# First attention of a two-layer decoder: the small matrix work of an iteration set beside the P*V products

## The chip, the cores and the metric

One NeuronCore of a Trainium2 chip runs the whole program. The metric is the device time of one execution in microseconds (us). Engines: TensorE (PE, matmuls; its weight loads are listed as PEld), VectorE (DVE), ScalarE (ACT), GpSimd (POOL), SyncE (SP, which here only issues DMAs).

## The reference

Eight sequences of 256 tokens with 128 channels go through two pre-norm layers of self-attention, cross-attention and a feed-forward part. The change touches the very first block, self-attention with 16 heads of 8 channels:

```python
x = x + _L0_attn_ref(_layernorm(x, axis=-1), W_qkv, b_qkv, W_out, b_out)
...
qkv = x @ W_qkv.T + b_qkv
q, k, v = jnp.split(qkv, 3, axis=-1)          # each to (B, 16 heads, 256, 8)
scores = jnp.einsum('bhqd,bhkd->bhqk', q, k) / jnp.sqrt(jnp.float32(HEAD_DIM))
att = jax.nn.softmax(scores, axis=-1)
out = jnp.einsum('bhqk,bhkd->bhqd', att, v)
return out.transpose(0, 2, 1, 3).reshape(B, T, D) @ W_out.T + b_out
```

The rest (cross-attention with one head, an expert block, causal attention, a second 16-head attention on the context, and a routed feed-forward part with a top-k) is the same in both kernels and runs after it.

## The kernel before

Every engine has its own program, written out by hand; nothing is scheduled by a tool. Semaphores tie them together. The kernel has three stages. The first 16-head attention (`lo == 0` in the code) goes over eight items, one sequence each. A middle stage does cross-attention, experts and causal attention. The second 16-head attention (`lo == B`) has the same loop as the first, over eight more items.

The loop of a 16-head attention is `for i ...: for h in range(16)`, and each engine walks it in the same order. At head h of iteration i TensorE issues, in `both_scores`, two kinds of scores turn by turn: the second scores of item i (L1324, `scores`, with the row maxima already folded in as an extra row of the stack) and the first scores of item i + 1 (L1333, `scores_for_max`), from which VectorE takes the maxima (L954, `row_max`). Both are bf16 matmuls on 62 or 63 rows of the array. The second scores of a head fill one of two banks and ScalarE's exponential (L658, `exps`) empties it; the first scores have three banks. These are the waits of the scores in `both_scores`, c and d being running numbers of heads:

```python
pe.wait_ge(exp_ready, c - 1)      # exponential of head h - 2 is done
pe.wait_ge(max_ready, d - 2)      # maxima of head h - 3 are done
```

Between the heads stands the rest of TensorE's work, in fp32:

- P*V (`weighted_sum`, L1370), 8 matmuls for four heads, each on 32 columns of the array: groups 0, 1, 2 at heads 5, 9, 13, group 3 at head 1 of the next iteration.
- For the item x = i + 3 that is being prepared: the transposes of its normalised input (`xn_transpose`, L1272), its q and k projections (`qk_project`, L1280 and L1284), its v projection (`v_project`, L1307). x runs from 3 to 9; items 8 and 9 already belong to the cross-attention and have only q (L1280).
- The transposes of the maxima (`max_transpose`, L1318), twice per item, at head 3 and for the next item at head 10.
- For item i - 1: transposes of the P*V result (`u_transpose`, L1383, head 3), of the normalised output (`o_transpose`, L1389, head 11), and the output projection (`out_project`, L1401, head 15).

ScalarE's list is, besides the exponentials: `max_copy` (L694) and the DMA that places the maxima in the stack (`place_max`, L700), `xnT_copy` (L668), `qk_copy` (L681), `v_copy` (L715), `u_copy` (L706), `oT_copy` (L752). `max_transpose`, `xn_transpose`, `qk_project` and `v_project` share one bank, `prep_ps`: each waits (`prep_free`) until ScalarE has copied the one before. After `qk_copy`, GpSimd splits q and k into bf16 parts and SyncE places them in the stack for iteration i + 2.

The heads at which these steps stand are numbers in the `if h == ...` lines. `at(lo, first, second)` gives one number for the first attention and another for the second.

Of the kernel before, what the change touches and what calls it, by code (L numbers as in the profile page):

```python
# [35 lines left out]
B, S, D = 8, 256, 128  # L36
# [39 lines left out]
CROSS, CAUSAL, LAST = 1, 2, 3  # L76
# [13 lines left out]
def build(nc, t):  # L90

    ctx = ExitStack()
    with ctx:
# [189 lines left out]
        def has(n, lo):  # L283

            return lo <= n < lo + B

        def layer(n):

            return WORK[n][0]
# [33 lines left out]
        def slot(n):  # L323

            return 2 if WORK[n][0] == LAST and n < MID_END else n % 2

        def before(n):

            return max((j for j in range(n) if slot(j) == slot(n)), default=None)

        def at(lo, first, second):

            return second if lo else first
# [318 lines left out]
        def _(act):  # L652
# [138 lines left out]
            for lo in MANY:  # L791
# [33 lines left out]
                for i in steps_of(lo):  # L825
                    x = prepared(i, lo)
                    for h in range(H):
                        if has(i, lo):
                            exps(i, h)
                        if h == 1 and has(i - 1, lo):  # L830
                            u_copy(i - 1)
                        if h == 3 and has(i, lo) and i != B:
                            max_copy(i, 1)
                        if h == 4 and has(i, lo) and i != B:
                            place_max(i, 1)
                        if h == at(lo, 3, 5) and x is not None:
                            xnT_copy(x)
                        for _ in range(KV_AT.get(i, ()).count(h)):
                            kv_copy(kv_done)
                            kv_done += 1  # L840
                        if h == at(lo, 7, 8) and x is not None:
                            qk_copy(x)
                        if (i, h) == (-3, 7):
                            value_biases()
                        if h == 11 and has(i + 1, lo):
                            max_copy(i + 1, 0)
                        if h == 12 and has(i + 1, lo):
                            place_max(i + 1, 0)
                        if h == 11 and has(i - 1, lo):
                            oT_copy(i - 1)  # L850
                        if h == 15 and x is not None and has(i + 3, lo):
                            v_copy(i + 3)
                        if h == 0 and lo == B and has(i - 3, lo):
                            xrT_copy(i - 3 - B)
# [404 lines left out]
        def _(pe):  # L1259
# [126 lines left out]
            def o_transpose(n):  # L1386
                pe.wait_ge(o_ready, n + 1)
                for k in range(NT):
                    i = pe.transpose(out_ps[:, k * P:(k + 1) * P], o_tok[:, n % 2, k, :], ident[:, :])  # L1389
                i.then_inc(oT_psum, 1)  # L1390
# [123 lines left out]
            for lo in MANY:  # L1514
# [55 lines left out]
                for i in steps_of(lo):  # L1570
                    x = prepared(i, lo)
# [7 lines left out]
                    for h in range(H):  # L1579
# [18 lines left out]
                            prep_free = (maxT_ready, 2 * i + 2)  # L1598
                        if h == 3 and has(i - 1, lo):
                            u_transpose(i - 1)  # L1600
                        if lo == 0 and h == 4 and x is not None:
                            if prep_free:
                                pe.wait_ge(*prep_free)
                            xn_transpose(x)
                            prep_free = (xnT_ready, x + 1)
                        if h % G == 1 and h >= G and has(i, lo):
                            weighted_sum(i, h // G - 1)
                        if lo == B and h == 5 and x is not None:
                            if prep_free:
                                pe.wait_ge(*prep_free)  # L1610
                            xn_transpose(x)
                            prep_free = (xnT_ready, x + 1)
                        if h == at(lo, 7, 8) and x is not None:
                            qk_project(x)
                            prep_free = (qk_ready, 2 * (x + 1))
                        if (i, h) == (-3, 7):
                            fold_matmul(0)
                        if (i, h) == (B - 1, 7) and lo == 0:
                            pe.wait_ge(*prep_free)
                            fold_matmul(1)  # L1620
                            prep_free = (bias_folded, 2)
                        if h == 11 and has(i - 1, lo):
                            o_transpose(i - 1)
                        if h == 10 and has(i + 1, lo):
                            if prep_free:
                                pe.wait_ge(*prep_free)
                            max_transpose(i + 1, 0)
                            prep_free = (maxT_ready, 2 * (i + 1) + 1)
                        for _ in range(KV_AT.get(i, ()).count(h)):
                            kv_project(kv_done)  # L1630
                            kv_done += 1
                        if h == 14 and x is not None and layer(x) != CROSS:
                            if prep_free:
                                pe.wait_ge(*prep_free)
                            v_project(x)
                            prep_free = (v_ready, v_count(x))
                        if h == 15 and has(i - 1, lo):
                            out_project(i - 1)
                        if h == 15 and lo == B and has(i - 2, lo) and i - 2 < lo + B - 1:
                            if prep_free:  # L1640
# [121 lines left out]
```

## Time and profile before

| | us |
|---|---|
| median of 3 runs | 397.46 (396.42 to 400.72) |
| profiled execution | 399.4 |
| its span | 397.6 |
| granted TensorE clock, mean | 0.985 of full |

The span goes from the first to the last instruction of the profiled execution; what lies around it is 1.8 us. All durations and start times in this text come from that one execution, start times counted from the span's start. "busy" of an engine is time in which it executes something; "idle before <-X" is time in which it stood still until X released it. A start time is the surest number of a matmul row: matmuls overlap, and their ends are modelled.

### The profile page before, as it was taken

To read this page: it belongs to the slowest core of one execution; us is meant where nothing else is said; L and a number is where in the kernel's file an instruction comes from. 1 tells how busy PE (TensorE), PEld (TensorE's weight loads), DVE (VectorE), ACT (ScalarE), POOL (GpSimd) and SP (SyncE) were. 2 spreads that over 40 slices of the span, in tenths; PEclk is the share of its full clock that TensorE was granted. 3 is DMA by queue.
4 is the path that set the end of the run, shared out by engine and by line. 5 is a ranking of instruction groups with operands and counts; after the bars stand their busy time and mean duration, and the time that the engine had idled before them with its cause. 6 is when DMAs were issued, how large, how long until landed. Compare 5 with 4: busy or idle time off the path is not lost.

```text
span 397.6 us, 9590 instructions
## 1 busy us (share of the span) xinstructions
PE 354.7 (89%) x3246; PEld 210.5 (53%) x3246; DVE 314.7 (79%) x874; ACT 265.6 (67%) x594; POOL 160.4 (40%) x267
## 2 busy tenths in 40 slices
PE   6889999999999889987887969999889899989994
PEld 6765444444444468775266834444444444447564
DVE  7778889989998277976367667898988997479995
ACT  3436888888878757767306666887777887765751
POOL 8425653565200023445006274157677422370001
PEclk9999999999999999999899898999999999999999
DMA  7442243224330000002000311311311300000003
GB/s 221 124 109 53 77 115 81 54 51 115 91 134 2 2 0 3 0 2 66 14 2 3 80 42 40 83 43 41 81 35 49 82 2 3 2 1 2 1 2 106
DMA packets 35830, 20.00 MB, mean 50 GB/s; under 512 B 4150, under 2 KB 34790, under 8 KB 35782
## 3 DMA queue, kind: packets, MB, share of 16 engines
q1 hardware_dynamic: 34982, 17.81, 16.9%
q10 hardware_dynamic: 608, 1.18, 0.8%
q8 instruction: 27, 0.44, 0.5%
q0 software_dynamic: 192, 0.39, 0.4%
q14 instruction: 21, 0.17, 0.1%
HBM read 5.58 MB, written 1.05 MB: 17 GB/s over the span
## 4 chain that ended last, share of the span: by engine, by line
PE 64%; DVE 13%; issue 6%; ACT 6%; POOL 5%; DMA 3%; SPq 2%; ACTq 0%; POOLq 0%; DVEq 0%
PE pv_ps L1370 15%; PE s_ps L1324 14%; PE s_ps L1427 4%; DVE negmax_sb L954 3%; PE prep_ps L1280 3%; PE s_ps L1333 3%; ACT probT_sb L658 3%; PE s_ps L1663 3%; PE out_ps L1482 2%; DVE xn_sb L938 2%; PE s_ps L1450 2%; PE prep_ps L1284 2%; PE s_ps L1510 2%; PE s_ps L1500 2%; PE out_ps L1401 2%
## 5 line engine op out<-in xcount | busy, mean ns | idle before, releaser
L954 DVE TENSOR_REDUCE negmax_sb<-s_ps 128x2 bf16<-128x512 f32 x256 | 163.9, 691 | 33.9 <-PE s_ps L1333 33.2
L658 ACT ACTIVATE probT_sb<-s_ps 128x512 f32<-128x512 f32 x256 | 143.3, 596 | 32.3 <-PE s_ps L1324 29.1
L1324 PE MATMUL s_ps<-stack_sb 63*128 63x256 bf16 x512 | 89.9, 273 | 11.1 <-ACT probT_sb L658 4.7
L1333 PE MATMUL s_ps<-stack_sb 62*128 62x256 bf16 x512 | 87.1, 274 | 6.0 <-DMA stack_sb<-parts_sb 4.6
L1370 PE MATMUL pv_ps<-probT_sb,v_aug_sb 128*32 128x256 f32 x1024 | 68.8, 386 | 0.5 <-ACT probT_sb L658 0.5
L1324 PEld LDWEIGHTS s_ps<-stack_sb 63*128 63x128 bf16 x512 | 30.8, 94 | 67.3 <-ACT probT_sb L658 38.2
L511 POOL TENSOR_SCALAR rstd_sb<-mv_sb 128x2 f32<-128x2 f32 x32 | 7.2, 225 | 100.5 <-DVE mv_sb L930 100.1
L1370 PEld LDWEIGHTS pv_ps<-probT_sb,v_aug_sb 128*32 128x32 f32 x1024 | 26.8, 109 | 25.9 <-issue 13.2
L1333 PEld LDWEIGHTS s_ps<-stack_sb 62*128 62x128 bf16 x512 | 29.6, 94 | 12.2 <-DMA stack_sb<-parts_sb 5.6
L681 ACT ACTIVATE qkf_sb<-prep_ps,b_qkv_sb 128x256 f32<-128x256 f32 x56 | 23.9, 470 | 13.7 <-PE prep_ps L1284 13.7
L938 DVE TENSOR_SCALAR xn_sb<-x_all_sb,mv_sb,rstd_sb 128x128 f32<-128x128 f32 x64 | 23.9, 465 | 3.8 <-POOL rstd_sb L513 3.6
L1192 DVE SCALAR_TENSOR_TENSOR late_sb<-late_sb,level_sb,k_inv_sb 8x256 f32<-8x256 f32 x49 | 23.2, 474 | 1.8
L513 POOL TENSOR_TENSOR rstd_sb<-rstd_sb,minus_half_sb 128x2 f32<-128x2 f32 x32 | 22.9, 716 | 2.7
L1280 PE MATMUL prep_ps<-xnT_sb,w_att_sb 128*128 128x256 f32 x64 | 21.9, 425 | 0.1
L407 POOL CAST parts_sb<-qkf_sb 128x512 bf16<-128x512 f32 x14 | 8.5, 609 | 29.9 <-ACT qkf_sb L681 29.9
L1427 PE MATMUL s_ps<-xrT_sb,d_w_sb 128*128 128x512 f32 x40 | 19.5, 611 | 0.8 <-ACT late_sb L746 0.8
L521 POOL TENSOR_TENSOR x_all_sb<-x_all_sb,b_vo_sb 128x256 f32<-128x256 f32 x16 | 11.5, 728 | 18.6 <-DVE xn_sb L938 18.5
L746 ACT ACTIVATE late_sb<-s_ps,d_b_sb 128x512 f32<-128x512 f32 x20 | 13.4, 686 | 6.1 <-PE s_ps L1427 6.1
L1007 DVE SCALAR_TENSOR_TENSOR x_all_sb<-out_ps,den_inv_sb,x_all_sb 128x128 f32<-128x128 f32 x32 | 9.8, 346 | 9.1 <-PE out_ps L1482 9.0
L412 POOL TENSOR_TENSOR parts_sb<-rest_sb,parts_sb 128x512 bf16<-128x512 f32 x14 | 16.2, 1160 | 1.1
L409 POOL TENSOR_TENSOR rest_sb<-qkf_sb,parts_sb 128x512 f32<-128x512 f32 x14 | 16.2, 1156 | 1.1
L410 POOL TENSOR_TENSOR parts_sb<-qkf_sb,parts_sb 128x512 bf16<-128x512 f32 x14 | 16.2, 1157 | 0.0
(206 smaller groups left out, 648.5 us busy)
## 6 DMA issues: line engine op xcount, KB each, us to landing
stack_sb<-parts_sb SPq DMA_DIRECT2D x186, 64.0 KB, 2.1
x_all_sb<-x SPq DMA_DIRECT2D x4, 256.0 KB, 3.3
ctxT_sb<-ctxT ACTq DMA_DIRECT2D x2, 512.0 KB, 6.6
f_w_sb<-f_w SPq DMA_DIRECT2D x2, 512.0 KB, 4.3
out<-x_all_sb SPq DMA_DIRECT2D x4, 256.0 KB, 2.4
d_w_sb<-d_w SPq DMA_DIRECT2D x2, 320.0 KB, 3.6
w_att_sb<-w_att SPq DMA_DIRECT2D x2, 256.0 KB, 4.0
stack_sb<-maxrow_sb ACTq DMA_DIRECT2D x32, 4.0 KB
```

The costliest lines, as they stand in the source:

```text
L409: eng.tensor_tensor(rest[:, :, :], qkf[:, w], parts[:, u, :, 0, :], ALU.subtract).then_inc(rest_ready, 1)
L513: pool.tensor_tensor(rstd[:, u, :], rstd[:, u, :], minus_half[:, 0:NT], ALU.pow).then_inc(rstd_ready, 1)
L658: act.activation(probT[:, c % 8], s2_ps[c % 2][:, :, :], ACT.Exp, scale=DH ** -0.5).then_inc(exp_ready, 1)
L681: act.activation(qkf[:, slot(n), a, :], prep_ps[:, a, :], ACT.Identity, bias=b_qkv[:, layer(n), a:a + 1]).then_inc(qk_ready, 2 if layer(n) ...
L938: i = dve.tensor_scalar(xn[:, u, k, :], x_all[:, tiles(n).start + k, :], mv[:, u, k, 0:1], rstd[:, u, k:k + 1], ALU.subtract, ALU.mult)
L954: dve.tensor_reduce(negmax[:, n % 2, :, max_column(max_head(h))], first_bank(c)[:, :, :], axis=AX.X, op=ALU.max, negate=True).then_inc(max ...
L1192: dve.scalar_tensor_tensor(out=min_junk[:, :], in0=e_row[:, :], scalar=level[:, a:a + 1], in1=k_inv[:, :], op0=ALU.min, op1=ALU.mult, accu ...
L1280: i = pe.matmul(prep_ps[:, 0, :], w_att[:, l, 0, :], xnT[:, u, :], start=True, stop=True)
L1324: i = pe.matmul(s2_ps[c % 2][:, k, :], stack[rows, s3, 1, h // 2, k * P:(k + 1) * P], stack[rows, s3, 0, h // 2, :], start=True, stop=True)
L1333: i = pe.matmul(first_bank(c)[:, k, :], stack[rows, s3, 0, hp, k * P:(k + 1) * P], stack[rows, s3, 1, hp, :], start=True, stop=True)
L1370: i = pe.matmul(pv_ps[0][32 * j:32 * j + 32, g // 2, :], v_cols[:, k, first:first + 32], probT[:, h % 8, k, :], start=(g % 2 == 0 and k == ...
L1427: pe.matmul(up_bank(c), d_w1[:, f, :], xrT[:, 2 * S * q:2 * S * (q + 1)], start=True, stop=True).then_inc(d_h_psum, 1)
```

## The change

A new helper gives a step's head for three cases: the second attention (`last`), iterations 0 to 7 of the first attention (`then`), and the three leading iterations -3 to -1 of the first attention (`early`). Only `then` differs from the numbers before, and `None` means not at all. In iterations 0 to 7 the transposes of xn move from head 4 to head 5, behind P*V 0; the q and k projections from 7 to 9, behind P*V 1; the transposes of the next item's maxima from 10 to 11, ahead of the transposes of the output; the v projection from 14 to 13 and the output projection from 15 to 13, both behind P*V 2. On ScalarE `xnT_copy` moves from 3 to 5, `qk_copy` from 7 to 9, `v_copy` from 15 to 14. By my count eleven places between heads become six (1, 3, 5, 9, 11, 13). VectorE, GpSimd and SyncE have the same programs in the same order.

```diff
+        def steady(i, lo, early, then, last):
+            return last if lo else then if i >= 0 else early
...
                         # ScalarE
-                        if h == at(lo, 3, 5) and x is not None:
+                        if h == steady(i, lo, 3, 5, 5) and x is not None:
                             xnT_copy(x)
-                        if h == at(lo, 7, 8) and x is not None:
+                        if h == steady(i, lo, 7, 9, 8) and x is not None:
                             qk_copy(x)
-                        if h == 15 and x is not None and has(i + 3, lo):
+                        if h == steady(i, lo, 15, 14, 15) and x is not None and has(i + 3, lo):
                             v_copy(i + 3)
...
                         # TensorE
-                        if lo == 0 and h == 4 and x is not None:
+                        if h == steady(i, lo, 4, None, None) and x is not None:
                             ...
                             xn_transpose(x)
                         if h % G == 1 and h >= G and has(i, lo):
                             weighted_sum(i, h // G - 1)
-                        if lo == B and h == 5 and x is not None:
+                        if h == steady(i, lo, None, 5, 5) and x is not None:
                             ...
                             xn_transpose(x)
-                        if h == at(lo, 7, 8) and x is not None:
+                        if h == steady(i, lo, 7, 9, 8) and x is not None:
                             qk_project(x)
-                        if h == 11 and has(i - 1, lo):
-                            o_transpose(i - 1)
-                        if h == 10 and has(i + 1, lo):
+                        if h == steady(i, lo, 10, 11, 10) and has(i + 1, lo):
                             ...
                             max_transpose(i + 1, 0)
+                        if h == 11 and has(i - 1, lo):
+                            o_transpose(i - 1)
-                        if h == 14 and x is not None and layer(x) != CROSS:
+                        if h == steady(i, lo, 14, 13, 14) and x is not None and layer(x) != CROSS:
                             ...
                             v_project(x)
-                        if h == 15 and has(i - 1, lo):
+                        if h == steady(i, lo, 15, 13, 15) and has(i - 1, lo):
                             out_project(i - 1)
```

The changed file is four lines longer, so its line numbers are higher by 4 (L1324 becomes L1328, and so on).

TensorE in iteration 1, before, from its q and k projections to P*V 1 (`pv_ps`): the heads are pairs of L1324 and L1333, two pairs to a head.

```order
L1280 MATMUL prep_ps<-xnT_sb,w_att_sb 128x256
L1284 MATMUL prep_ps<-xnT_sb,w_att_sb 128x256
L1324 MATMUL s_ps<-stack_sb 128x256
L1333 MATMUL s_ps<-stack_sb 128x256
L1324 MATMUL s_ps<-stack_sb 128x256
L1333 MATMUL s_ps<-stack_sb 128x256
L1324 MATMUL s_ps<-stack_sb 128x256
L1333 MATMUL s_ps<-stack_sb 128x256
L1324 MATMUL s_ps<-stack_sb 128x256
L1333 MATMUL s_ps<-stack_sb 128x256
L1370 MATMUL pv_ps<-probT_sb,v_aug_sb 32x256 x8
```

The same engine and place after the change, from head 8 to the q and k projections:

```order
L1328 MATMUL s_ps<-stack_sb 128x256
L1337 MATMUL s_ps<-stack_sb 128x256
L1328 MATMUL s_ps<-stack_sb 128x256
L1337 MATMUL s_ps<-stack_sb 128x256
L1374 MATMUL pv_ps<-probT_sb,v_aug_sb 32x256 x8
L1284 MATMUL prep_ps<-xnT_sb,w_att_sb 128x256
L1288 MATMUL prep_ps<-xnT_sb,w_att_sb 128x256
```

The projections stood ahead of heads 8 and 9; now those heads come straight after heads 6 and 7, and the projections follow P*V 1.

TensorE in iteration 1, before, from P*V 2 to the output projection (L1401):

```order
L1370 MATMUL pv_ps<-probT_sb,v_aug_sb 32x256 x8
L1324 MATMUL s_ps<-stack_sb 128x256
L1333 MATMUL s_ps<-stack_sb 128x256
L1324 MATMUL s_ps<-stack_sb 128x256
L1333 MATMUL s_ps<-stack_sb 128x256
L1307 MATMUL prep_ps<-w_att_sb,xnT_sb 128x128 x2
L1324 MATMUL s_ps<-stack_sb 128x256
L1333 MATMUL s_ps<-stack_sb 128x256
L1324 MATMUL s_ps<-stack_sb 128x256
L1333 MATMUL s_ps<-stack_sb 128x256
L1401 MATMUL out_ps<-w_att_sb,oT_sb 128x128 x2
```

The same place after the change:

```order
L1374 MATMUL pv_ps<-probT_sb,v_aug_sb 32x256 x8
L1311 MATMUL prep_ps<-w_att_sb,xnT_sb 128x128 x2
L1405 MATMUL out_ps<-w_att_sb,oT_sb 128x128 x2
L1328 MATMUL s_ps<-stack_sb 128x256
L1337 MATMUL s_ps<-stack_sb 128x256
L1328 MATMUL s_ps<-stack_sb 128x256
L1337 MATMUL s_ps<-stack_sb 128x256
```

The v projection (L1307, now L1311) and the output projection have moved up behind P*V 2, and heads 14 and 15 now stand before heads 0 and 1 of the next iteration with nothing between them.

ScalarE in iteration 1, before, from `xnT_copy` at head 3 (L668) to `v_copy` at head 15 (L715); L658 are exponentials:

```order
L668 ACTIVATE xnT_sb<-prep_ps 128x256
L658 ACTIVATE probT_sb<-s_ps 128x512
L700 DMA stack_sb<-maxrow_sb 2x4x256
L658 ACTIVATE probT_sb<-s_ps 128x512 x3
L681 ACTIVATE qkf_sb<-prep_ps,b_qkv_sb 128x256 x2
L658 ACTIVATE probT_sb<-s_ps 128x512 x4
L694 ACTIVATE maxrow_sb<-prep_ps 8x256
L752 ACTIVATE oT_sb<-out_ps 128x256
L658 ACTIVATE probT_sb<-s_ps 128x512
L700 DMA stack_sb<-maxrow_sb 2x4x256
L658 ACTIVATE probT_sb<-s_ps 128x512 x3
L715 ACTIVATE v_aug_sb<-prep_ps 128x32x8
```

and after the change, from exponential 5 to `v_copy` at head 14:

```order
L662 ACTIVATE probT_sb<-s_ps 128x512
L672 ACTIVATE xnT_sb<-prep_ps 128x256
L662 ACTIVATE probT_sb<-s_ps 128x512 x4
L685 ACTIVATE qkf_sb<-prep_ps,b_qkv_sb 128x256 x2
L662 ACTIVATE probT_sb<-s_ps 128x512 x2
L698 ACTIVATE maxrow_sb<-prep_ps 8x256
L756 ACTIVATE oT_sb<-out_ps 128x256
L662 ACTIVATE probT_sb<-s_ps 128x512
L704 DMA stack_sb<-maxrow_sb 2x4x256
L662 ACTIVATE probT_sb<-s_ps 128x512 x2
L719 ACTIVATE v_aug_sb<-prep_ps 128x32x8
```

`xnT_copy` (L668, now L672) comes behind exponential 5 instead of ahead of exponential 4, `qk_copy` (L681, now L685) behind exponential 9 instead of 7, and `v_copy` behind exponential 14.

## Rows read from the trace of the kernel before

**Rows 1.** The page of the profile, part 1: busy time by engine.

```profile
PE 354.7 (89%) x3246; PEld 210.5 (53%) x3246; DVE 314.7 (79%) x874; ACT 265.6 (67%) x594; POOL 160.4 (40%) x267
```

**Rows 2.** Window of iteration 3: its length, then busy PE, PEld, DVE, ACT, POOL.

```profile
76.60:89.90 13.30, 13.11 (x155) 6.45 (x156) 12.17 (x26) 11.28 (x25) 7.11 (x9) 1.00 0.24 62
```

**Rows 3.** Waits from 33.7 to 137.6 us: us in total, times, longest us.

```profile
PEld s_ps L1324 <- ACT probT_sb L658: 19.7, 58, 0.7
...
ACT probT_sb L658 <- PE s_ps L1324: 9.6, 26, 0.9
```

**Rows 4.** Timeline of TensorE, iteration 3: start us, us, instruction.

```profile
76.61 0.28 PE L1324 MATMUL s_ps<-stack_sb 63*128 63x256 bf16 x1
...
77.19 0.41 PE L1272 MATMUL prep_ps<-ident_sb,xn_sb 128*128 128x128 f32 x2 [0.19 <-ACT maxrow_sb L694]
77.53 0.28 PE L1324 MATMUL s_ps<-stack_sb 63*128 63x256 bf16 x1
...
77.85 1.07 PE L1370 MATMUL pv_ps<-probT_sb,v_aug_sb 128*32 128x256 f32 x16
78.86 0.28 PE L1324 MATMUL s_ps<-stack_sb 63*128 63x256 bf16 x1
...
79.09 0.27 PE L1324 MATMUL s_ps<-stack_sb 63*128 63x256 bf16 x1
...
79.40 0.70 PE L1280 MATMUL prep_ps<-xnT_sb,w_att_sb 128*128 128x256 f32 x2
...
81.00 1.07 PE L1370 MATMUL pv_ps<-probT_sb,v_aug_sb 128*32 128x256 f32 x16
...
83.94 1.07 PE L1370 MATMUL pv_ps<-probT_sb,v_aug_sb 128*32 128x256 f32 x16
...
85.26 0.71 PE L1307 MATMUL prep_ps<-w_att_sb,xnT_sb 128*128 128x128 f32 x4
...
86.23 0.71 PE L1401 MATMUL out_ps<-w_att_sb,oT_sb 128*128 128x128 f32 x4
...
87.42 1.07 PE L1370 MATMUL pv_ps<-probT_sb,v_aug_sb 128*32 128x256 f32 x16
...
89.88 0.28 PE L1324 MATMUL s_ps<-stack_sb 63*128 63x256 bf16 x1
```

**Rows 5.** Timeline of ScalarE in the same iteration.

```profile
75.78 1.08 ACT L658 ACTIVATE probT_sb<-s_ps 128x512 f32<-128x512 f32 x2
...
79.28 1.08 ACT L658 ACTIVATE probT_sb<-s_ps 128x512 f32<-128x512 f32 x2 [0.28 <-PE s_ps L1324]
80.57 0.84 ACT L681 ACTIVATE qkf_sb<-prep_ps,b_qkv_sb 128x256 f32<-128x256 f32 x2 [0.20 <-PE prep_ps L1284]
81.30 2.27 ACT L658 ACTIVATE probT_sb<-s_ps 128x512 f32<-128x512 f32 x4
...
86.83 0.38 ACT L715 ACTIVATE v_aug_sb<-prep_ps 128x256 f32<-128x256 f32 x1
87.30 1.09 ACT L658 ACTIVATE probT_sb<-s_ps 128x512 f32<-128x512 f32 x2
```

**Rows 6.** Chain of waits in iteration 7: start us, us, what.

```profile
133.20 0.38 PE s_ps L1324 x4
...
134.05 0.60 ACT probT_sb L658
...
134.70 0.39 PE s_ps L1324 x2
```

**Rows 7.** Timeline of TensorE in the second attention, around a P*V at head 5.

```profile
251.37 1.07 PE L1370 MATMUL pv_ps<-probT_sb,v_aug_sb 128*32 128x256 f32 x16
252.38 0.44 PE L1272 MATMUL prep_ps<-ident_sb,xn_sb 128*128 128x128 f32 x2
...
253.87 0.27 PE L1324 MATMUL s_ps<-stack_sb 63*128 63x256 bf16 x1 [0.51 <-ACT probT_sb L658]
```

**Rows 8.** Chain of waits between iterations 6 and 7: the longest transfer of the maxima.

```profile
110.11 3.06 DMA stack_sb<-maxrow_sb
```

## The prediction

> **What bounds the kernel now.** I read the page first: TensorE is busy for 354.7 of 397.6 us, VectorE for 314.7, ScalarE for 265.6 [rows 1]. Such shares are means over unlike stages, so next came a window over one whole iteration of the first attention (i = 3, 76.6 to 89.9): 13.30 us, with TensorE 13.11 busy, VectorE 12.17, ScalarE 11.28 [rows 2]. Three engines are nearly full, each feeding the next. The waits of the whole first attention show how they hold each other: the scores (L1324) wait for the exponentials (L658) 58 times, 19.7 us in total at their weight loads, and the exponentials for the scores 26 times, 9.6 us [rows 3]. So what counts is the ring between TensorE and ScalarE. There are two banks for the second scores: those of head h wait until the exponential of head h-2 has left its bank. What stands between two heads on TensorE is free as long as it fits into that wait.
>
> The timeline of TensorE in iteration 3 [rows 4] is the ruler. I count from the scores of head 4 (76.61). The products P*V (L1370) of groups 0, 1, 2 start at 1.24, 4.39, 7.33, the last group (issued at head 1 of the next iteration) at 10.81, and the next head 4 at 13.27. Other prices: from P*V to what follows 1.01 (77.85 to 78.86); q and k projections 1.06 (from 79.40 to P*V 1 at 81.00 there are 1.60, of which two heads take 0.54); v projection 0.65 (85.26 to 86.23 holds it and a head of 0.32); output projection 0.64 by the same pattern; a head with nothing behind it 0.23 (78.86 to 79.09), and 0.32 where another kind of matmul follows (77.53 to 77.85).
>
> From ScalarE's timeline [rows 5]: an exponential starts 0.42 after its head's scores (79.28 after 78.86), the next 0.54 later (two take 1.08); the copy of the q, k projection starts 1.17 after the projection (80.57) and holds ScalarE for 0.73 (next exponential 81.30); the copy of v pushes the next exponential by 0.47 (86.83 to 87.30).
>
> The important row is of iteration 7, where nothing large stands between two P*V groups: four heads, begun at 133.20, let the next P*V start at 135.09 (the last scores on the chain, 134.70 and 0.39 long, end where it starts) [rows 6]. That is **1.89 us for four heads in a row**, although TensorE's own share is some 0.23 + 0.23 + 0.23 + 0.32 = 1.0. The scores at 134.70 follow the exponential that began at 134.05, 0.65 earlier. The second attention shows it with the maxima running too: behind a P*V and the transposes joined to it (252.38) two heads go out, and the third waits until 253.87 for an exponential, TensorE idle for 0.51 [rows 7].
>
> **The change part by part.** The instructions stay the same; only places change, in iterations 0 to 7 of the first attention. Per iteration with a self-attention item (i = 0 to 4, x = 3 to 7):
>
> 1. Head 4 to P*V 1. Before 4.39: the transposes of xn waited for the copy of the maxima (0.19 idle at 77.19) and stood in a place of their own. Now heads 4 and 5 are adjacent. Head 5 waits only for exponential 3, the second of the pair begun at 75.78 [rows 5], so at 76.32: with 0.65 this is 0.36 on my ruler. P*V 0 follows at 0.68, the transposes at 1.69, head 6 at 2.04 (the transposes take 0.34, 77.19 to 77.53). Heads 6 to 9 are now four in a row: 1.89, and 0.05 because the copy of xn stands ahead of exponential 6. P*V 1 starts at 3.98: **-0.4**.
> 2. P*V 1 to head 10. Before 1.01 to head 10 (at 5.40 on the ruler); now the q and k projections stand behind it: 1.01 + 1.06. **+1.06**. Before, these 1.06 filled the wait between heads 7 and 8: heads 6 to 9 with the projections took from 78.86 to 81.00, 2.14 [rows 4], against 1.89 without them.
> 3. Head 10 to P*V 2. Before 1.93. ScalarE waits in order for q and k: the copies start 0.11 after head 10's scores and last 0.73, so exponential 10 starts at 0.84 instead of 0.42, exponential 11 at 1.39, head 13 at 2.04, P*V 2 at 2.36. The transposes of the maxima now at head 11 wait for the same copies (their bank is shared), inside this time. **+0.43**.
> 4. P*V 2 to the last P*V. Before 3.48, with v behind head 14 and the output projection behind head 15, both in the ring's waits. Now both stand behind P*V 2: 1.01 + 0.65 + 0.64 = 2.30, then heads 14, 15, 0, 1 in a row, 1.89, and the copy of v, placed between exponentials 14 and 15, adds its 0.47: 4.66 to 4.70. **+1.2**.
> 5. The last P*V to the next head 4: same instructions, 2.46. **0**.
>
> Sum 2.3, less 0.08 because the copy of u comes in closer: **+2.2 us**, five times: 11.1. The queues behind are not late: SyncE's stack loads start after the q, k copy and GpSimd's split, both 2.2 later, and their deadline, two iterations on, moves by more.
>
> Iterations 5 and 6 prepare cross-attention items: q alone (0.70 long by the row at 79.40 [rows 4], some 0.63 to what follows), one copy, no v. q uncovered +0.63, output projection uncovered +0.64, less 0.4 of part 1, plus some 0.2 of part 3: +1.1 each, 2.2. Iteration 7 has only the output projection moved: +0.6. **In all +13.9 us.** The profiled execution took 399.4 us (span 397.6), 1.9 over the median of 397.46, so 413.3 for a profiled one and **411.4** for the median.
>
> What the joins save on TensorE is in those numbers. A change of kind costs 0.09: a head takes 0.32 instead of 0.23 when other matmuls follow. The joined P*V and transposes of the second attention start 1.01 apart (251.37 to 252.38), the same as P*V to scores, so a join with P*V still pays one such step. A full iteration has six such steps fewer (three at head 13, one each at heads 5, 9 and 11), 0.54 us. The Trainium skill says the same (TensorEngine Tiling (Array Packing), "Key Properties"): changing the tiling mode drains the engine, while changing the tile within it does not. The scores are 64-row tiles, P*V 32-column ones, the projections use the full array. By that page alone the change only saves drains and would end faster, as in the first rival; the 0.09 of the trace agrees that a change of mode costs something.
>
> **The rivals.** (a) *TensorE's own time decides, faster.* It is busy 13.11 of 13.30, and the chain runs through it. Then each iteration loses the 0.54 of the six steps and 0.25 of waiting for the maxima's copy (head 4 to the transposes 0.58 against 0.32), 0.8 over seven iterations 5.5 us, 392; VectorE's 12.17 is the floor, 7.7 us or 390 at the most. It decides if, after a joined group, the third head's scores are already released. Against it: two banks hold two heads, whatever TensorE does before, and rows 6 and 7 show the third waiting. Chance 0.06. The Trainium skill's rule on draining, named above, speaks for this rival.
> (b) *The lost cover is half returned.* ScalarE idles in the long group at head 13, so the copy of v and the maxima may be out of the way and heads 14 to 1 go at TensorE's own pace, 1.0 instead of 1.89 + 0.47. Part 4 is then 2.30 + 1.0 - 3.48 = -0.2, an iteration 0.9 to 1.1 longer, and the time 404 to 406. For it: ScalarE is busy 11.28 of 13.30 only. Against it: the ring is a matter of order, not of sums [rows 6]. Chance 0.13.
> (c) *The row of the maxima comes late.* Its transfer took 3.06 us once [rows 8]. Head 8 now comes 3.1 after head 4 instead of 3.85, and the issue stands at about 0.5: 0.5 + 3.06 = 3.56. Up to 0.5 per iteration, part of it behind exponential 7: +0.7 to +3.5 us, 412 to 415. Chance 0.15.
> (d) Gains and losses cancel, within 1% (about what a measurement of this kernel can tell from no change): 0.05.
> Likeliest: as summed, 408 to 414, 0.61.
>
> **How the numbers follow.** Slower by over 1% (above 401.4) are the likeliest case, (b) and (c): 0.89. Faster 0.06, the same 0.05. The range leaves out (a) and (d) and a little beyond either end: 403 to 416.5. The ring's price is known best; the copy of v (0.47, or nothing if it found a gap) gives 2.4 us downwards, late maxima 3 upwards.
>
> **What the profile would show.** Iterations of 15.3 to 15.6 us from head 4 to head 4 (i = 0 to 4), and some 14.1 for i = 5 and 6. Scores with 0.3 to 0.8 idle before them at heads 8, 9, 0 and 1, released by exponentials; ScalarE and VectorE idle for 1 to 2 us while P*V 1 + q, k and P*V 2 + v + output run; the q, k copy right after head 10's scores go out. TensorE's sum of busy time all but unchanged, its share lower. The second attention unchanged. I am wrong if the heads 8 and 14 to 1 follow at 0.23, or if the four heads after a joined group take clearly less than 1.89.

## The result, and the profile after

The changed kernel takes 408.8 us (median of 4 runs, 407.7 to 411.9) against 399.1 us (396.4 to 400.9, 4 runs): a ratio of **1.0256, interval 1.0208 to 1.0305, slower**. Its profiled execution took 408.85 us, span 407.0.

One iteration of the first attention in the changed kernel, as a window (columns as in [rows 2]):

```profile
66.40:81.43 15.03, 13.19 (x154) 6.50 (x154) 12.00 (x26) 11.10 (x25) 7.12 (x9) 1.00 0.24 62
```

The iteration has grown from 13.27 to 15.03 us while each engine is about as busy as before (TensorE 13.19, VectorE 12.00, ScalarE 11.10). So each of them has 1.7 to 1.9 us more of idle time, though not at the same moments: VectorE and ScalarE stand still while TensorE works through its long groups, and TensorE stands still while they work. On TensorE's timeline (start us, us, instruction, idle before) the same points as in [rows 4]:

```profile
66.40 0.28 PE L1328 MATMUL s_ps<-stack_sb 63*128 63x256 bf16 x1
...
67.11 1.07 PE L1374 MATMUL pv_ps<-probT_sb,v_aug_sb 128*32 128x256 f32 x16
68.11 0.44 PE L1276 MATMUL prep_ps<-ident_sb,xn_sb 128*128 128x128 f32 x2
...
69.60 0.27 PE L1328 MATMUL s_ps<-stack_sb 63*128 63x256 bf16 x1 [0.51 <-ACT probT_sb L662]
...
70.43 1.07 PE L1374 MATMUL pv_ps<-probT_sb,v_aug_sb 128*32 128x256 f32 x16
71.43 0.70 PE L1284 MATMUL prep_ps<-xnT_sb,w_att_sb 128*128 128x256 f32 x2
...
73.49 0.28 PE L1322 MATMUL prep_ps<-ident_bf_sb,negmax_sb 128*8 128x128 bf16 x2 [0.38 <-ACT qkf_sb L685]
...
74.79 1.07 PE L1374 MATMUL pv_ps<-probT_sb,v_aug_sb 128*32 128x256 f32 x16
75.79 0.71 PE L1311 MATMUL prep_ps<-w_att_sb,xnT_sb 128*128 128x128 f32 x4
76.33 0.61 PE L1405 MATMUL out_ps<-w_att_sb,oT_sb 128*128 128x128 f32 x4
76.88 0.28 PE L1328 MATMUL s_ps<-stack_sb 63*128 63x256 bf16 x1
...
78.00 0.27 PE L1328 MATMUL s_ps<-stack_sb 63*128 63x256 bf16 x1 [0.51 <-issue]
...
78.72 0.28 PE L1328 MATMUL s_ps<-stack_sb 63*128 63x256 bf16 x1 [0.33 <-ACT probT_sb L662]
...
79.04 1.07 PE L1374 MATMUL pv_ps<-probT_sb,v_aug_sb 128*32 128x256 f32 x16
```

Both runs of four heads stall at their third head (69.60, 78.00), the second run again at its fourth (78.72), and the transposes of the maxima wait 0.38 for the copy of q and k. The other two engines, in the same iteration, ScalarE first:

```profile
72.60 0.84 ACT L685 ACTIVATE qkf_sb<-prep_ps,b_qkv_sb 128x256 f32<-128x256 f32 x2 [1.48 <-PE prep_ps L1288]
...
77.30 0.60 ACT L662 ACTIVATE probT_sb<-s_ps 128x512 f32<-128x512 f32 x1 [1.43 <-PE s_ps L1328]
77.80 0.38 ACT L719 ACTIVATE v_aug_sb<-prep_ps 128x256 f32<-128x256 f32 x1
78.06 1.68 ACT L662 ACTIVATE probT_sb<-s_ps 128x512 f32<-128x512 f32 x3
80.18 0.60 ACT L710 ACTIVATE uT_sb<-pv_ps 128x512 f32<-128x512 f32 x1 [0.44 <-PE pv_ps L1374]
```

and VectorE:

```profile
68.67 3.08 DVE L958 TENSOR_REDUCE negmax_sb<-s_ps 128x2 bf16<-128x512 f32 x5
72.95 1.29 DVE L958 TENSOR_REDUCE negmax_sb<-s_ps 128x2 bf16<-128x512 f32 x2 [1.20 <-PE s_ps L1337]
74.52 1.29 DVE L958 TENSOR_REDUCE negmax_sb<-s_ps 128x2 bf16<-128x512 f32 x2 [0.28 <-PE s_ps L1337]
77.34 1.30 DVE L958 TENSOR_REDUCE negmax_sb<-s_ps 128x2 bf16<-128x512 f32 x2 [1.52 <-PE s_ps L1337]
```

VectorE is idle for 1.20 + 0.28 + 1.52 = 3.00 us, all of it behind the two long groups of TensorE and the wait for the copy. From the maxima of head 14 to those of head 9 in the next iteration (77.34 to 86.8, 9.4 us) it works without a break, while ScalarE has gaps in that stretch too (0.44 at 80.18). This was not in the prediction, and the experiments below had to deal with it.

As the measure of the experiments I take the **length of the first attention**, from the first second scores of iteration 0 to the first matmul of the middle stage. It is 104.8 us before (33.77 to 138.59) and 115.9 after (33.67 to 149.59): +11.1. It leaves out what varies between executions: the start (33.6 to 36.6 us in these profiles), and TensorE's clock in the later stages. Each length comes from one profiled execution. Its iterations repeat closely (15.03, 15.02, 15.03 us), but two kernels below whose first attention is the same program have 101.7 and 101.9 us, so differences of 0.2 to 0.3 us tell nothing by themselves. One profile, of half exponentials in the old order, is of a slow execution; its clock in the first attention is 1.00 as in all others, and nothing outside the first attention is taken from it.

The span grew by only 9.4 us. Windows of before (first row) and of after (second), both begun where the second attention has come equally far:

```profile
236.00:242.00 6.00, 4.32 (x30) 2.11 (x30) 3.78 (x8) 2.75 (x7) 1.21 (x2) 0.74 0.36 89
```

```profile
247.00:253.00 6.00, 4.31 (x50) 2.03 (x46) 4.98 (x13) 3.45 (x8) 1.24 (x3) 1.00 0.36 90
```

The granted clock (third column from the right) was 0.74 in the mean here before, so part of the time at 1.2 GHz, and 1.00, 2.4 GHz, after; the matmuls that got done in the 6 us are 30 and 50. From the transposes of xn in these windows (237.27 and 248.28) to the head behind the next P*V (242.98 and 252.46) the same work took 5.71 us before and 4.18 after. These 1.5 us are nearly all of the 1.7 between +11.1 and +9.4. In the first attention the clock is 1.00 in both.

### The profile page after: what moved, and what is told of

Its sections match the earlier page's. It is cut to its first block, busy times and chain, and to the rows that moved or that the text cites. A ratio compares the mean times of both kernels' runs of the same rounds, so it can differ in the third digit from the quotient of the medians.

```text
span 407.0 us, 9590 instructions
## 1 busy us (share of the span) xinstructions
PE 353.7 (87%) x3246; PEld 209.9 (52%) x3246; DVE 313.6 (77%) x874; ACT 265.8 (65%) x594; POOL 160.4 (39%) x267
## 4 chain that ended last, share of the span: by engine, by line
PE 61%; DVE 16%; issue 7%; ACT 7%; POOL 5%; SPq 2%; DMA 1%; ACTq 0%; POOLq 0%; DVEq 0%
PE pv_ps L1374 13%; PE s_ps L1328 12%; DVE negmax_sb L958 6%; PE s_ps L1431 4%; ACT probT_sb L662 3%; PE prep_ps L1284 3%; PE s_ps L1667 3%; DVE xn_sb L942 2%; PE out_ps L1486 2%; PE s_ps L1454 2%; PE s_ps L1337 2%; PE s_ps L1504 2%; PE s_ps L1514 2%; PE out_ps L1405 2%; PE prep_ps L1288 2%
## 5 line engine op out<-in xcount | busy, mean ns | idle before, releaser
L1328 PE MATMUL s_ps<-stack_sb 63*128 63x256 bf16 x512 | 88.6, 272 | 20.0 <-ACT probT_sb L662 8.9
L1328 PEld LDWEIGHTS s_ps<-stack_sb 63*128 63x128 bf16 x512 | 31.7, 94 | 72.1 <-ACT probT_sb L662 34.9
L1374 PEld LDWEIGHTS pv_ps<-probT_sb,v_aug_sb 128*32 128x32 f32 x1024 | 26.7, 109 | 26.2 <-issue 12.8
L685 ACT ACTIVATE qkf_sb<-prep_ps,b_qkv_sb 128x256 f32<-128x256 f32 x56 | 23.9, 471 | 20.7 <-PE prep_ps L1288 18.5
```

The source lines that it names most:

```text
L685: act.activation(qkf[:, slot(n), a, :], prep_ps[:, a, :], ACT.Identity, bias=b_qkv[:, layer(n), a:a + 1]).then_inc(qk_ready, 2 if layer(n) ...
L1328: i = pe.matmul(s2_ps[c % 2][:, k, :], stack[rows, s3, 1, h // 2, k * P:(k + 1) * P], stack[rows, s3, 0, h // 2, :], start=True, stop=True)
L1374: i = pe.matmul(pv_ps[0][32 * j:32 * j + 32, g // 2, :], v_cols[:, k, first:first + 32], probT[:, h % 8, k, :], start=(g % 2 == 0 and k == ...
```

## The experiments

All comparisons are with the kernel before on the same chip. The diffs are against the changed kernel, whose lines read `steady(i, lo, early, then, last)`.

### One part at a time

Only the q and k projections moved:

```diff
 # xnT_copy, xn_transpose, max_transpose, v_project, out_project, v_copy: numbers of before
                         if h == steady(i, lo, 7, 9, 8) and x is not None:
                             qk_project(x)       # and qk_copy(x) on ScalarE
```

> One part of the change alone: in iterations 0 to 7 only the q and k projections and their copy move, from head 7 to head 9 behind P*V 1; all else as before. Ring theory (four heads in a row take 1.89 us, and the projections lose that cover): P*V 1 0.25 us earlier, +1.06 behind it, +0.43 because exponential 10 waits for the copies, so +1.2 us in each of iterations 0 to 4 and +0.6 in 5 and 6, the first attention 7.2 us longer, a ratio of 1.018. Rival (TensorE's own time and its changes of mode decide): one step of 0.09 less per iteration, 0.6 us shorter, ratio 0.998.

Measured: ratio 1.0241 (1.0204 to 1.0278); first attention 114.4 us, **+9.6**. The direction is the ring theory's, the size 2.4 us above it. TensorE's timeline of this kernel:

```profile
71.27 0.27 PE L1328 MATMUL s_ps<-stack_sb 63*128 63x256 bf16 x1 [0.51 <-ACT probT_sb L662]
72.04 1.07 PE L1374 MATMUL pv_ps<-probT_sb,v_aug_sb 128*32 128x256 f32 x16
73.04 0.70 PE L1284 MATMUL prep_ps<-xnT_sb,w_att_sb 128*128 128x256 f32 x2
75.10 0.27 PE L1322 MATMUL prep_ps<-ident_bf_sb,negmax_sb 128*8 128x128 bf16 x2 [0.61 <-ACT qkf_sb L685]
76.70 1.07 PE L1374 MATMUL pv_ps<-probT_sb,v_aug_sb 128*32 128x256 f32 x16
```

With the transposes of the maxima still at head 10, they wait 0.61 for the bank that q and k hold, and head 11 waits behind them: from P*V 1 to P*V 2 4.66 us, in the changed kernel 4.36. Moving the maxima to head 11 is thus worth 0.30 us per iteration where q and k were moved. Where they were not, it is worth 0.05: in the third kernel of this section P*V 1 to P*V 2 takes 2.89 us, before 2.94.

Only v and the output projection moved:

```diff
 # all else: numbers of before
                         if h == steady(i, lo, 14, 13, 14) and x is not None and layer(x) != CROSS:
                             v_project(x)
                         if h == steady(i, lo, 15, 13, 15) and has(i - 1, lo):
                             out_project(i - 1)
```

> The other large part alone: the v projection moves from head 14 to 13 and the output projection from 15 to 13, both behind P*V 2, and the copy of v from 15 to 14. Ring theory, with the prices that the changed kernel showed (P*V 2 to head 14 2.09, the four heads 2.16): 4.25 instead of 3.48 us, +0.8 in iterations 0 to 4, +0.0 to 0.6 in 5 and 6, +0.6 in 7: the first attention 5.1 us longer, ratio 1.013. Rival (TensorE's own time): three steps of 0.09 less per iteration, 1.9 us shorter, ratio 0.995.

Measured: ratio 1.0105 (1.0052 to 1.0158); first attention 109.8 us, **+5.0** against 5.1 expected.

Only the two small joins:

```diff
 # q, k, v, output projection and their copies: numbers of before
                         if h == steady(i, lo, None, 5, 5) and x is not None:
                             xn_transpose(x)
                         if h == steady(i, lo, 10, 11, 10) and has(i + 1, lo):
                             max_transpose(i + 1, 0)
```

> The two small parts together: the transposes of xn behind P*V 0 (head 5) with their copy, and the transposes of the maxima at head 11 joined with those of the output; q, k, v and the output projection as before. Ring theory: neither makes four heads follow each other without cover, since the q and k projections still stand between heads 7 and 8; P*V 1 comes 0.2 us earlier and one step of 0.09 goes, -0.3 us per iteration, 2 us shorter, ratio 0.995. Rival (every join costs, since ScalarE's copies move too): +0.2 per iteration, ratio 1.003.

Measured: ratio 0.9926 (0.9896 to 0.9957); first attention 103.0 us, **-1.8**. So the change holds a part that gains and two that lose. The three sum to +12.8, 1.7 more than the whole, most of it the wait for the bank just shown (0.3 in each of five iterations).

### Is a run of four heads a wait that takes work for nothing?

The changed kernel with two matmuls whose result nobody reads, once between heads 7 and 8, once in the joined group:

```diff
+                        if lo == 0 and i >= 0 and h == 7 and x is not None:   # 13 in the other
+                            pe.wait_ge(*prep_free)
+                            filler(2)          # 128 x 128, fp32, into prep_ps
```

> The changed kernel with two idle fp32 matmuls (128 x 128, result unused) put between heads 7 and 8 of iterations 0 to 6, where TensorE now waits 0.5 us for exponential 6. Ring theory: they fill the wait; with 0.54 us and two changes of mode (0.18) against a slack of 0.66 they cost 0.1 us per iteration at most, the first attention up to 0.5 us longer. Rival (TensorE's own time decides): 0.7 us per iteration, 5 us.

Measured: ratio to before 1.026 (1.0159 to 1.036); first attention 115.9 us, **+0.0** against the changed kernel.

> The same two matmuls, but behind P*V 2 at head 13, inside the joined group, where by the ring theory nothing hides them (both other engines already stand idle there). Ring theory: 0.54 us in each of seven iterations, the first attention 3.8 us longer than in the changed kernel. Rival (TensorE's own time decides): about the same as for the filler between heads 7 and 8, 3.8 to 5 us.

Measured: ratio to before 1.0368 (1.0275 to 1.0461); first attention 119.0 us, **+3.1**, 0.44 per iteration. The timelines show the same four records (L1274) at the two places, between heads 7 and 8 first:

```profile
69.06 0.71 PE L1274 MATMUL prep_ps<-ident_sb 128*128 128x128 f32 x4
69.70 0.28 PE L1333 MATMUL s_ps<-stack_sb 63*128 63x256 bf16 x1
```

```profile
64.11 0.71 PE L1274 MATMUL prep_ps<-ident_sb 128*128 128x128 f32 x4
64.65 0.61 PE L1316 MATMUL prep_ps<-w_att_sb,xnT_sb 128*128 128x128 f32 x4
65.10 0.61 PE L1410 MATMUL out_ps<-w_att_sb,oT_sb 128*128 128x128 f32 x4
```

Between the heads they take 0.64 us including the changes of mode, and head 8 starts at 69.70, with no idle before it; P*V 1 follows P*V 0 by 3.32 us as without them. In the joined group, with matmuls of their own kind behind them, they lengthen the way from P*V 2 to head 14 by 0.45 us (2.54 instead of 2.09), and the iteration by 0.44. The same work costs nothing in one place and its length in the other: this is what was done to q, k, v and the output projection. It speaks against the first rival, that TensorE's own time decides.

### Which engine holds the run?

The exponentials over half of the columns, in both kernels:

```diff
-                act.activation(probT[:, c % 8], s2_ps[c % 2][:, :, :], ACT.Exp, ...)
+                act.activation(probT[:, c % 8, 0], s2_ps[c % 2][:, 0, :], ACT.Exp, ...)   # 8 <= c < H * B
```

> The changed kernel with the exponentials of the first attention (from head 8 of iteration 0 on) taken over half of the columns only; the other half of the probabilities is left as it was in the buffer, so the output is not the reference's. It is to be read beside the same edit of the kernel before. If the ring of ScalarE alone makes the runs of four heads slow, the iteration falls from 15.0 to below 13.7 us, and the changed kernel is at most 0.5 us per iteration slower than the kernel before with the same edit. If VectorE's maxima (one per 0.61 us, three banks) stand right behind it, the iteration falls only to 14.3 to 14.5 us.

> The kernel before with the same exponentials over half of the columns (output not the reference's). Ring theory and its rivals agree on the size: TensorE's own work holds the iteration at 12.6 to 13.1 us instead of 13.27. The difference to the changed kernel with the same edit is what tells: 0.5 us or less per iteration if ScalarE alone made the loss, 1.3 to 1.8 if VectorE would make it as well.

Measured: first attention 112.4 and 101.0 us, a **loss of 11.4**, as with whole exponentials (11.1). ScalarE alone does not make it; my ring theory, as written, fell here. The iteration takes 14.84 us in the new order, longer than either forecast, and 13.09 in the old. Behind ScalarE stands VectorE: the first scores of head h wait for the maxima of head h - 3. Heads 8 and 9 and the maxima of heads 5 to 9 in the new order with half exponentials:

```profile
70.23 0.27 PE L1331 MATMUL s_ps<-stack_sb 63*128 63x256 bf16 x1 [0.58 <-ACT probT_sb L663]
70.83 0.27 PE L1331 MATMUL s_ps<-stack_sb 63*128 63x256 bf16 x1 [0.20 <-DVE negmax_sb L961]
```

```profile
69.40 3.08 DVE L961 TENSOR_REDUCE negmax_sb<-s_ps 128x2 bf16<-128x512 f32 x5
```

The first row names ScalarE, but the view names the signal that came last, whoever was needed. The signals' times in the packed trace say more. Head 8 needs exponential 6, which begins at 69.47 and takes 0.38, and the maxima of head 5, which are ready at 70.09: it waits for the maxima. In the changed kernel the maxima of head 5 are ready at 69.37 and exponential 6 at 69.51, and head 8 starts at 69.60. So there the exponential holds it, and the maxima were ready 0.14 us earlier; at head 9 they are 0.03 apart (69.97 and 70.00). In the run of heads 14 to 1 the exponential is the later one by far (78.67 against 78.05 at head 1). What half exponentials gain there, 3.83 us instead of 4.25 from P*V 2 to the last P*V, is mostly lost again up to P*V 1, where the maxima hold.

So the maxima were halved as well:

```diff
+                w = S // 2 if 0 < n < B else S
-                dve.tensor_reduce(..., first_bank(c)[:, :, :], axis=AX.X, op=ALU.max, ...)
+                dve.tensor_reduce(..., first_bank(c)[:, :, 0:w], axis=AX.X, op=ALU.max, ...)
```

> The kernel before with both ends of the rings shortened in the first attention: exponentials over half of the columns, and the maxima over half of the columns too (items 1 to 7), so the output is not the reference's. TensorE's work stays. It is the measure for the same edit of the changed kernel. With 13.27 us per iteration before, of which TensorE works 13.1, both theories expect 12.6 to 13.0.

> The changed kernel with the same two edits. Half the exponentials alone left the loss where it was (11.4 us against 11.1), so the ring of ScalarE alone is not the cause. Two-ring theory (a run of four heads is held either by the exponentials or by the maxima, whichever is later): with both short the runs pass at TensorE's pace, only the wait for the copy of q and k (0.4 us) and the uncovered tail stay, and the loss against the kernel before with the same edits falls from 11 to 2 to 5 us. Rival (the joined groups themselves cost it, by their length on TensorE or by the bank of the copies): the loss stays at 9 to 11 us.

Measured: first attention 99.6 and 106.8 us, a **loss of 7.2**: between the two forecasts. One iteration each as a window, before (first) and after:

```profile
66.25:79.04 12.79, 12.79 (x155) 6.59 (x153) 8.44 (x26) 8.10 (x25) 7.11 (x9) 1.00 0.26 67
```

```profile
66.38:80.14 13.76, 12.67 (x154) 6.70 (x152) 8.13 (x26) 8.11 (x25) 7.08 (x10) 1.00 0.23 59
```

The old order keeps TensorE busy for 12.79 of 12.79 us. The new order has 0.12 less work for it and 1.1 us of idle time: 0.39 at the wait for the copy of q and k, 0.30 at the third head of each of the two runs of four, and some 0.1 at the fourth head of the second run, behind the copy of v. VectorE and ScalarE, with 8.1 us each, are far from full, and still the new order loses 1 us. The third head waits because the way to ScalarE and back is long even for a short exponential. In the first run head 6 starts at 67.75, its exponential at 68.17, behind the copy of xn; it takes 0.38, and head 8 starts at 68.66: 0.91 us, in which TensorE has two heads of work. So the waits that are left stand in the same places as those of the changed kernel; halving both engines' work takes 3.9 of the 11.1 us of loss away. The maxima alone were not halved, so how much of the 3.9 VectorE would give by itself is not shown.

### The copy of v

```diff
-                        if h == steady(i, lo, 15, 14, 15) and x is not None and has(i + 3, lo):
+                        if h == steady(i, lo, 15, 13, 15) and x is not None and has(i + 3, lo):
                             v_copy(i + 3)
```

> The changed kernel with the copy of v at head 13 on ScalarE, in the idle time while the joined group runs, instead of behind exponential 14. Ring theory: the run of heads 14 to 1 shrinks from 2.16 to 1.89 us, five times: 1.3 us shorter than the changed kernel. Rival (the copy was covered anyway; the maxima hold these heads): no change, within 0.2 us.

Measured: ratio to before 1.0288 (1.0253 to 1.0323); first attention 115.7 us, **-0.25** against the changed kernel, all of it in iteration 0; the iterations behind it take 15.03 us as before. That is the rival's side. The run of heads 14 to 1 did become shorter: P*V 2 to the last P*V 3.98 instead of 4.25 us. It was given back in the next run, as TensorE's timeline of this kernel shows at heads 8 and 9:

```profile
85.91 0.27 PE L1328 MATMUL s_ps<-stack_sb 63*128 63x256 bf16 x1 [0.58 <-DVE negmax_sb L958]
86.51 0.27 PE L1328 MATMUL s_ps<-stack_sb 63*128 63x256 bf16 x1 [0.20 <-DVE negmax_sb L958]
```

The releaser is now the maxima. VectorE's gaps stay as they were (1.20, 0.27 and 1.52 us, behind the long groups and the wait for the copy), and so does the iteration. Twice the exponentials' side was loosened, and twice the maxima held the heads instead.

### Joining without runs of four

```diff
 # q and k at head 7, out_project and v_copy at 15 as before;
 # xn_transpose at 5, max_transpose at 11 as in the changed kernel
-                        if h == steady(i, lo, 14, 13, 14) and x is not None and layer(x) != CROSS:
+                        if h == steady(i, lo, 14, 15, 14) and x is not None and layer(x) != CROSS:
                             v_project(x)
```

> A version that joins without making runs of four heads: as e3_xn_max_only, and the v projection moves from head 14 to 15, where it stands with the output projection between heads 15 and 0 (copy of v at 15 as before). Ring theory: two heads, group, two heads; P*V 2 to the last P*V takes 1.01 + 0.23 + 0.32 + 1.08 + 0.55 = 3.19 instead of 3.48, so -0.6 us per iteration with e3's part, 3 to 4 us shorter in all, ratio 0.991. Rival (VectorE, 12.17 of 13.27 busy, becomes the bound or starves in the joined group): no faster than e3, ratio 0.995 to 1.000.

Measured: 395.4 us, ratio **0.9897 (0.9861 to 0.9934)**; first attention 101.7 us, -3.1. That is 1% faster than before, clear of the interval. The joined group in its timeline, and one of its iterations as a window:

```profile
56.36 1.07 PE L1374 MATMUL pv_ps<-probT_sb,v_aug_sb 128*32 128x256 f32 x16
57.91 0.71 PE L1311 MATMUL prep_ps<-w_att_sb,xnT_sb 128*128 128x128 f32 x4
58.46 0.61 PE L1405 MATMUL out_ps<-w_att_sb,oT_sb 128*128 128x128 f32 x4
59.54 1.07 PE L1374 MATMUL pv_ps<-probT_sb,v_aug_sb 128*32 128x256 f32 x16
```

```profile
63.90:76.60 12.70, 12.67 (x154) 6.49 (x152) 12.10 (x25) 11.16 (x24) 7.12 (x9) 1.00 0.27 69
```

P*V 2 to the last P*V takes 3.18 us (3.19 expected, 3.48 before). Every run has two heads, TensorE is busy for 12.67 of 12.70, and VectorE with 12.10 sits 0.6 below. The v and output projections take 0.55 + 0.54 us here, as in the changed kernel, and nothing is uncovered.

The same with the maxima of the second attention at head 11 too:

```diff
-                        if h == steady(i, lo, 10, 11, 10) and has(i + 1, lo):
+                        if h == steady(i, lo, 10, 11, 11) and has(i + 1, lo):
                             max_transpose(i + 1, 0)
```

> The paired version (xn transposes behind P*V 0, maxima with the output's transposes at head 11, v and output projection together at head 15, q and k left at head 7), and in the second attention the transposes of the maxima moved from head 10 to 11 as well, to share a place with the output's transposes. Two-ring theory: one step of 0.09 to 0.18 less in seven iterations of the second attention, 0.6 to 1.3 us shorter than the paired version, ratio to before 0.987. Rival (VectorE, then the bound of the second attention): the same as the paired version, 0.990.

Measured: ratio 0.9907 (0.987 to 0.9943), no different from the paired version. The traces show a small gain where the change was made: from the first to the last transposes of u of the second attention 97.6 us, in the paired version 98.0. That is less than the 0.6 to 1.3 forecast, and too little for the ratio to show. What limits it was not looked into.

## Why the prediction was right, and where it was off

The forecast was slower, 411.4 us in 403 to 416.5; measured 408.8. It said +13.9 us, the median moved by 9.7, the first attention by 11.1. The two totals lie closer than the two differences, and that part is luck: the median of the kernel before was 397.46 when the forecast was added to it, and with a fourth run it is 399.09. The forecast of the iteration, 15.3 to 15.6 us, was missed (15.03). By its own steps, for the iteration from 66.40 on, against that of [rows 4]:

- **Step 1, head 4 to P*V 1.** Forecast 3.98 us, measured 4.03. P*V 0 starts at 0.71 (0.68 forecast), and TensorE is idle for 0.51 before head 8, as in [rows 7].
- **Step 2, P*V 1 to head 10.** Forecast 2.07, measured 2.06 (70.43 to 72.49, a row not shown; the projections start 1.00 after P*V 1).
- **Step 3, head 10 to P*V 2.** Forecast 2.36, measured 2.30. The copy of q and k starts 0.11 after head 10, and the transposes of the maxima wait 0.38 for it.
- **Step 4, P*V 2 to the last P*V.** Forecast 4.66 to 4.70, measured 4.25. **This is the mis-sized term**, 0.45 of the 0.46 us by which the iteration's sum is too long, some 2.2 of the 2.8 us. One half is the joined pair of projections: 0.65 + 0.64 taken as if alone, while together they take 75.79 to 76.88, 1.09. The prediction says that the saved changes of mode are in its numbers; the two between these projections are not. The other half is the copy of v: 0.47 was read between two exponentials [rows 5] of which the second had to wait for its scores. What the copy itself pushes is 77.80 to 78.06, 0.26, near its 0.38 less the overlap.
- **Step 5, the last P*V to head 4.** Forecast 2.46 less 0.08, measured 2.39.
- **The price of four heads in a row**, 1.89, held (1.95 for heads 6 to 9 with the copy of xn among the exponentials; 1.89 for heads 14 to 1 once the copy of v is out of them, 78.25 to 80.14 in that kernel's trace). The row it was read from is not as bare as the prediction says: the transposes of the output stand between its heads, at 133.46. They lie inside the wait, so the price is the same.
- **Iterations 5 to 7** were forecast at +1.1, +1.1 and +0.6, together 2.8. Counted from one group of transposes of u to the next, they took 12.99, 12.40 and 11.62 us before and take 13.86, 13.55 and 12.25: +0.9, +1.15 and +0.6, together 2.65. Iterations 0 to 4 hold the other 8.4, where 11.1 was forecast.
- From 11.1 us in the first attention to 9.7 in the medians: in the two profiles the clock in the second attention makes such a difference, 1.5 us. The interval of the ratio, 8.3 to 12.2 us, holds the 11.1.

The **mechanism** was right in what it said of cover: the filler matmuls cost nothing between heads 7 and 8 and their length in the group. It was incomplete in naming ScalarE. I took the ring of two banks as the one that holds, and VectorE's 12.17 only as a floor for the rival. In fact both rings hold at nearly the same distance at heads 8 and 9 (69.37 and 69.51 at head 8). So half exponentials (-3.5 us in the new order, -3.8 in the old, the loss unchanged) and the earlier copy of v (-0.25 instead of -1.3) left the loss standing. The numbers came out well all the same because in the changed kernel the exponential is the later of the two at that head, by 0.14 us; the sum looked at one ring only, and that VectorE's gives nearly the same length was luck.

Of the rivals: (a), TensorE's own time, is refuted for the long groups, but its 0.09 per change of mode is real: two matmul groups of the same mode in a row save 0.2 us (1.09 against 1.29), the small joins gained 1.8 us, and small joins and paired projections together 3.1. The Trainium skill's rule on draining (TensorEngine Tiling (Array Packing), "Key Properties") says that changing the tiling mode drains TensorE, and the traces agree, with a limit to what a join can save: P*V, on 32 columns, to transposes of the full array is a change of mode too, and at 67.11 to 68.11 no shorter than P*V to scores. (b), half of the cover returned, would be step 4 at -0.2; it was +0.8. (c), late maxima, had no part in the iterations shown. The transfer is issued at 66.99 and its signal comes at 68.58, a microsecond ahead of head 8, so it took 1.6 us and not the 3.06 of [rows 8]. In the next iteration the weight loads of head 8 name the transfer as their releaser, but there too its signal (83.98) comes ahead of the exponential's (84.54). The matmul that does wait for it, in iteration 5, waits 0.78 us at 122.19, and its counterpart before, at 113.21, waited 0.75.

## What to carry to other kernels

- Work that stands in a wait of a pipeline is free up to the length of the wait. Before it is moved to save something, read how long the consumer engines need for the items that now become neighbours: here, with two banks, the third neighbour already stalled, for 0.51 us.
- Joins paid here where they kept the distance of the fed engines even: two heads, group, two heads. Joining two groups of the same tiling mode saved 0.2 us; what stands behind a P*V starts no earlier for the join.
- When three engines are nearly full, loosening one ring can show nothing. Busy and idle time add up to the iteration for every engine (VectorE 12.0 + 3.0, ScalarE 11.1 + 3.9), so the sum doesn't name the one that holds; where the gaps lie is of more help. VectorE's lie only behind TensorE's long groups and the copy, none in the runs of heads. A releaser's name in a row is a hint: compare the times of all signals that the instruction needs.

## What the runs showed of the hardware

The v or output projection, four records of fp32 128 x 128 matmuls, takes 0.64 to 0.65 us to the next start with bf16 scores on either side, 0.54 to 0.55 with matmuls of its own mode on one side (75.79 to 76.33, 76.33 to 76.88), and 0.45 with them on both (64.65 to 65.10 in the kernel with idle matmuls in the joined group). So entering and leaving the mode cost about 0.1 us each.

TensorE's granted clock can differ between executions in a stretch with the same instructions. At the start of the second attention it was 0.74 in the mean of 6 us in one profile and 1.00 in the other. In both TensorE had been idle for 1.22 us just before the transposes at 237.27 and 248.28, and for 0.47 and 0.46 us two heads later. Then the q and k projections have records of 1.22 and 1.06 us at the lower clock, 0.70 and 0.59 at the full one.
